# Attention scores and their maxima as products of 64 array rows, two heads side by side, in a fused attention and mixture-of-experts kernel

## What is computed

```
x = x + tanh(g_xattn) * attention(layernorm(x), ctx, ctx)
    scores = q_h . k_h / 4          (per head h, 256 x 77; keys beyond the query position masked)
    attn   = softmax(scores);  out = attn . v_h;  out @ W.T + b
x = x + tanh(g_ffn) * ffn(layernorm(x))
    shared = swiglu(x @ w_in.T) @ w_out.T
    h      = swiglu(x @ w1.T)
    routed = sum over the two chosen experts e:  (h * weight_e) @ w2[e].T
```

## Time and profile before

| | |
|---|---|
| median of 3 executions | 1141.14 us (1137.15 to 1141.66) |
| profiled execution | 1138.31 us, span of its instructions 1136.6 us |
| mean granted TensorE clock | 0.986 |
| PE busy | 1084.2 us, 95% of the span |
| weight loads busy | 908.4 us, 80% |
| DVE busy | 818.2 us, 72% |
| POOL busy | 520.0 us, 46% |
| ACT busy | 472.3 us, 42% |

### The profile page before, as it was taken

The page is one execution under the profiler, slowest core; times in us unless marked ns, Lnnn a source line. Parts: engine busy times, 40 slices in busy tenths (PEclk is TensorE's granted clock), DMA queues, the critical chain, the costliest instruction groups (busy, mean ns, idle before and its releaser), DMA issues.

```text
span 1136.6 us, 22381 instructions
## 1 busy us (share of the span) xinstructions
PE 1084.2 (95%) x7411; PEld 908.4 (80%) x7411; DVE 818.2 (72%) x1810; ACT 472.3 (42%) x722; POOL 520.0 (46%) x644
## 2 busy tenths in 40 slices
PE   5689999999999999999999999999999999999997
PEld 3467888888788787788888777888887888888886
DVE  7757786886876876877878676557544688888886
ACT  4565556555555555655555432233221111111111
POOL 5334447457357456465563534000001566666564
PEclk8989999999999999999999999999999899999999
DMA  8975748666765764766666112687652554555451
GB/s 157 244 159 120 147 102 129 135 126 102 146 137 123 119 146 106 113 141 128 99 128 145 29 55 74 209 260 242 214 173 104 163 157 154 163 166 150 148 175 64
DMA packets 106162, 160.64 MB, mean 141 GB/s; under 512 B 28828, under 2 KB 70718, under 8 KB 106048
## 3 DMA queue, kind: packets, MB, share of 16 engines
q1 hardware_dynamic: 94276, 121.18, 46.8%
q0 software_dynamic: 11776, 38.03, 11.1%
HBM read 75.24 MB, written 52.10 MB: 112 GB/s over the span
## 4 chain that ended last, share of the span: by engine, by line
PE 71%; issue 11%; DVE 7%; POOL 6%; DMA 3%; ACT 2%; SPq 1%; POOLq 0%; DVEq 0%; ACTq 0%
PE ps L764 16%; PE ps L811 12%; PE ps L709 7%; PE ps L726 7%; PE ps L813 6%; PE ps L631 4%; PE ps L796 3%; PE ps L619 3%; PE ps L662 2%; POOL tab_dram L1471 2%; PE ps L585 2%; PE ps L589 2%; POOL x L1447 2%; DMA regr<-regr 2%; PE ps L640 1%
## 5 line engine op out<-in xcount | busy, mean ns | idle before, releaser
L811 PE MATMUL ps<-regr,gh 128*128 x600 | 221.6, 407 | 0.2 <-issue 0.2
L888 ACT ACTIVATE Pt<-ps,pbias 77x1024 f32<-77x1024 f32 x128 | 141.6, 1106 | 98.2 <-PE ps L619 96.8
L813 PE MATMUL ps<-regr,gl 128*128 x600 | 170.0, 283 | 0.0
L811 PEld LDWEIGHTS ps<-regr,gh 128*128 128x128 f32 x600 | 113.8, 190 | 23.9 <-issue 0.6
L978 ACT ACTIVATE gh<-ps 128x512 fp32r<-128x512 f32 x75 | 44.8, 599 | 204.9 <-PE ps L796 204.9
L1189 DVE TENSOR_REDUCE mneg<-ps 128x8 f32<-128x616 f32 x128 | 100.4, 792 | 21.3 <-PE ps L589 21.1
L813 PEld LDWEIGHTS ps<-regr,gl 128*128 128x128 f32 x600 | 114.0, 190 | 0.0
L709 PE MATMUL ps<-x2h,winh 128*128 128x512 f32 x256 | 108.2, 423 | 0.6 <-DVE OHR L1093 0.6
L1379 POOL TENSOR_TENSOR gl<-gf,gh 128x512 fp32r<-128x512 f32 x64 | 82.7, 1293 | 42.8 <-ACT gh L850 42.6
L1447 POOL TENSOR_TENSOR x<-x,regf 128x512 f32<-128x512 f32 x32 | 41.1, 1285 | 132.7 <-DMA x<-in_x 132.7
L709 PE MATMUL ps<-x2h,winl 128*128 128x512 f32 x256 | 100.6, 393 | 0.0
(11 more groups left out here) (201 smaller groups left out, 2652.9 us busy)
## 6 DMA issues: line engine op xcount, KB each, us to landing
regr<-regr SPq DMA_DIRECT2D x96, 256.0 KB, 5.9
y_dram<-Pt SPq DMA_DIRECT2D x64, 256.0 KB, 2.4
regf<-in_x SPq DMA_DIRECT2D x32, 256.0 KB, 4.3
x<-in_x SPq DMA_DIRECT2D x32, 256.0 KB, 7.2
y_dram<-res SPq DMA_DIRECT2D x32, 256.0 KB, 2.4
regr<-regr SPq DMA_DIRECT2D x96, 77.0 KB, 6.9
x_dram<-x2h SPq DMA_DIRECT2D x14, 512.0 KB, 3.0
x_dram<-x2l SPq DMA_DIRECT2D x14, 512.0 KB, 3.8
```

The costliest lines, as they stand in the source:

```text
L811: e.matmul(o, gh2[:, k % 3, fc, :], w2v[:, bass.ds(val, 1), fc, :, :].rearrange("p o h d -> p (o h) d"), start=fc == 0, stop=False, skip_g ...
L813: m = e.matmul(o[:, 0, :], gl2[:, k % 3, fc, :], w2v[:, bass.ds(val, 1), fc, 0, :].rearrange("p o d -> p (o d)"), start=False, stop=fc == ...
L888: e.activation(Pt[0:K, 4 * k:4 * k + 4, :].rearrange("k (n j) t -> k n (j t)", n=2), bank_of["sc", b, k][0:K, :, :], ACT.Exp, bias=pbias[: ...
```

## The change

**Layout.** The 128 partitions are split into a lower and an upper half of 64, and head j of each pair lives in half j: `Kst` and `Xs` hold 50 rows from partition 64j (queries high, high, low in three blocks of 16, two rows of maxima), `Kbd` needs 4 instead of 8 heads per copy, and `mcat` is reordered.

**Maxima.** Each product has 64 rows (a half) and 308 columns; the two halves write separate banks. For the first half of the positions (k < 2) the mask still comes by the identity with 128 rows, now first; for k >= 2 it comes by `sel`, a matrix with a one in partitions 0 and 64, also in halves. A stage `mask` takes the banks, and waits for them, in slot 2k; `max` now stands in slot 2k+1, ahead of `scores`, and PE holds its products back until the causal masks of that `scores` stage are issued, so that products of 64 rows follow each other.

**Scores.** The four products of 100 rows become four of 50 rows, alternately in the lower and the upper half, the two heads in separate banks. ACT reads and writes in the new order, with one instruction as before.

**Transfers.** The three of `queries` become six, of half the size, the one of `maxT` becomes two. The ones in `Kst` are set once by POOL at the start, in place of a transfer with a copy on ACT and two clears on DVE.

```
-        put(i - 1, ((0, "max", 0), (0, "max", 1), (0, "max", 2), (0, "max", 3), (3, "maxT", 0)) if i < 6 else
-            ((0, "max", 0), (2, "max", 1), (4, "max", 2), (6, "max", 3), (9, "maxT", 0)))
+        put(i - 1, [(0, n, k) for k in range(4) for n in ("mask", "max")] + [(3, "maxT", 0)] if i < 6 else
+            [(2 * k + j, n, k) for k in range(4) for j, n in enumerate(("mask", "max"))] + [(9, "maxT", 0)])
...
                     for r, t in enumerate((xTh, xTh, xTl)):
-                        dst = Xs[32 * r:32 * r + 32, h, :, :, :].rearrange("p q c t -> p (q c t)")
-                        e.dma_start(dst.bitcast(F), t[:, h, :, :].bitcast(F)).then_inc(s[f"xs{h}"], 16)
+                        for j in range(2):
+                            o = 64 * j + 16 * r
+                            dst = Xs[o:o + 16, h, :, :, :].rearrange("p q c t -> p (q c t)")
+                            e.dma_start(dst.bitcast(F), t[64 * j:64 * j + 64, h, :, :].bitcast(F)).then_inc(s[f"xs{h}"], 16)
...
+            def maxima(b, k):
+                t, c = k // 2, k % 2
+                o = bank_of["mm", b, k][:, :, 0:4 * K].rearrange("p q (h k) -> p q h k", h=4)
+                if t:
+                    for j in range(2):
+                        e.matmul(o[:, j], sel[64 * j:64 * j + 64, :],
+                                 pad[64 * j:64 * j + 64, b, :].unsqueeze(1).broadcast_to([64, 4, K]), start=True, stop=False)
+                for j in range(2):
+                    m = e.matmul(o[:, j], xTh[64 * j:64 * j + 64, b % 2, c, t * P:(t + 1) * P],
+                                 Kbd[64 * j:64 * j + 64, b % G, c, :, :], start=False, stop=True)
+                m.then_inc(s["mm"], 1)
...
-                elif stage_ == "max":
+                elif stage_ == "mask":
...
                     bk, (sem, v) = take("P", "mm", b, k)
                     e.wait_ge(sem, v)
...
+                    if k < 2:
+                        for j in range(2):
+                            e.matmul(o[:, j], identb[:, :], first[:, h, :].unsqueeze(1).broadcast_to([P, 4, K]), start=True, stop=False)
+                elif stage_ == "max":
+                    if b < 5:
+                        maxima(b, k)
+                    else:
+                        maxima_due.append((b, k))
...
+                    while maxima_due:
+                        maxima(*maxima_due.pop())
                     for n in range(2):
-                        p, bk = 2 * k + n, pair[:, n, :]
+                        p = 2 * k + n
                         for j in range(2):
-                            m = e.matmul(bk[0:K, j * S:(j + 1) * S], Kst[:, ks, j, p % 4, 2 * g + p // 4, :],
-                                         Xs[:, h, p % 4, p // 4, :], start=False, stop=j == 1, skip_group_check=True)
+                            m = e.matmul(pair[0:K, j, n * S:(n + 1) * S], Kst[64 * j:64 * j + KR, ks, p % 4, 2 * g + p // 4, :],
+                                         Xs[64 * j:64 * j + KR, h, p % 4, p // 4, :], start=False, stop=n == 1, skip_group_check=True)
...
+            e.memset(sel[:, :], 0.0).then_inc(s["gcon"], 1)
+            e.wait_ge(s["gcon"], GCON["sel_zero"])
+            for j in range(2):
+                e.memset(Kst[64 * j + 32:64 * j + 64, :, :, :, :].bitcast(F), 1.0).then_inc(s["gcon"], 1)
...
-                    e.tensor_tensor(Kbd[:, b % G, k, :, :], khi[:, b % G * 2 + k, :].bitcast(F).unsqueeze(1).broadcast_to([P, 8, K]),
-                                    own8[:, :].unsqueeze(2).broadcast_to([P, 8, K]), ALU.mult).then_inc(s["kbd"], 1)
+                    e.tensor_tensor(Kbd[:, b % G, k, :, :], khi[:, b % G * 2 + k, :].bitcast(F).unsqueeze(1).broadcast_to([P, 4, K]),
+                                    own4[:, :].unsqueeze(2).broadcast_to([P, 4, K]), ALU.mult).then_inc(s["kbd"], 1)
```

More of the change, by code:

```diff
@@ L17 @@
 G = 2
-KR = 100
+KR = 50
 HID = 512
@@ L38 @@
 DCON = {n: i + 1 for i, n in enumerate(
-    "idb m8 ks0 va_zero va_one ones rec pre_zero pre wgh0 lb0 tgh brow pbias crow kcol ks1".split())}
-GCON = {n: i + 6 for i, n in enumerate("ident caus cauT upb kint".split())}
+    "idb m4 va_zero va_one ones rec pre_zero pre wgh0 lb0 tgh brow pbias crow kcol".split())}
+GCON = {n: i + 6 for i, n in enumerate("ident caus cauT upb kint sel_zero ones_low kst sel_low sel".split())}
 ROUTES = [(4 * c - 4, 8, c) for c in range(1, NCH - 2, 2)] + [(4 * c, 4, c) for c in (NCH - 2, NCH - 1)]
@@ L294, in build @@
         klo = carve(P, [2 * G, K])
-        Kbd = carve(P, [G, 2, 8, K])
+        Kbd = carve(P, [G, 2, 4, K])
         xTh = carve(P, [2, 2, S])
         xTl = carve(P, [2, 2, S])
-        w1_at = used[0]
+        w1_at = used[0] = max(used[0], 4096)
         kf = carve(P, [2 * G, K], regf)
@@ L574, in tensor @@
                     m.then_inc(s["xT"], 1)
-                elif stage_ == "max":
+                elif stage_ == "mask":
                     if k == 0:
                         e.wait_ge(s["xTh"], b + 1)
-                    t, c = k // 2, k % 2
-                    e.wait_ge(s["kbd"], 2 * b + c + 1)
+                        e.wait_ge(s["first"], b + 1)
+                    if b == 0 and k == 2:
+                        e.wait_ge(s["gcon"], GCON["sel"])
+                    e.wait_ge(s["kbd"], 2 * b + k % 2 + 1)
                     bk, (sem, v) = take("P", "mm", b, k)
@@ L582, in tensor @@
                     o = bk[:, :, 0:4 * K].rearrange("p q (h k) -> p q h k", h=4)
-                    for q in range(2):
-                        e.matmul(o[:, q], xTh[:, h, c, t * P:(t + 1) * P], Kbd[:, g, c, 4 * q:4 * q + 4, :], start=True, stop=False)
-                    if k == 0:
-                        e.wait_ge(s["first"], b + 1)
-                    for q in range(2):
-                        m = e.matmul(o[:, q], identb[:, :], (pad[:, b, :] if t else first[:, h, :]).unsqueeze(1).broadcast_to([P, 4, K]),
-                                     start=False, stop=True)
-                    m.then_inc(s["mm"], 1)
+                    if k < 2:
[6 more added lines that the diff above has]
+                        maxima_due.append((b, k))
                 elif stage_ == "maxT":
@@ L1404, in gpsimd @@
             e.iota(kint[:, :], pattern=[[0, 1]], base=0, channel_multiplier=1).then_inc(s["gcon"], 1)
+            e.memset(sel[:, :], 0.0).then_inc(s["gcon"], 1)
+            e.wait_ge(s["gcon"], GCON["sel_zero"])
+            for j in range(2):
+                e.memset(Kst[64 * j + 32:64 * j + 64, :, :, :, :].bitcast(F), 1.0).then_inc(s["gcon"], 1)
+                e.wait_ge(s["gcon"], GCON["ones_low"] + j)
+            for j in range(2):
+                e.memset(sel[64 * j:64 * j + 1, :], 1.0).then_inc(s["gcon"], 1)
+            e.wait_ge(s["gcon"], GCON["sel"])
             for stage_, b, k in order:
@@ L1538 @@
         _np.diff([p_[0] for p_ in pairs]), _np.diff([p_[1] for p_ in pairs])]).astype(_np.float32)
-    own = _np.zeros((4, 2, H, K), _np.float32)
-    for r_ in range(4):
-        own[r_, r_ % 2] = 1.0
-    arrays["own"] = own.reshape(4, -1)
     nc = _bacc.Bacc("TRN2", target_bir_lowering=False, num_devices=1)
```

70 lines of the change are left out of this document (28 added, 42 removed), and 2 rows, old and new, of the table names.

## The result

| | before | after |
|---|---|---|
| median | 1139.26 us (1135.84 to 1142.70, 6 runs) | 1198.27 us (1196.55 to 1200.22, 6 runs) |
| profiled execution, span | 1138.31, 1136.6 us | 1197.72, 1196.0 us |
| mean granted TensorE clock | 0.986 | 0.965 |

The ratio is 1.0501, 95% interval 1.0468 to 1.0534. The change costs 59 us. I had forecast 1170 us, with 1140 to 1190 as the range: the direction was right, the size was not, and the time lies outside the range.

The account below looks back on a forecast made before the run. Phase one looked bound by PE (494 of 500 us busy), with a late DVE reduction deciding. Profiled 1138.3 + 41 (waits) - 6 (PE) - 4 (values) + 2 (start) = 1171 us; predicted 1170, range 1140 to 1190.

Parts of the forecast that it names:

- forecast 0.8: PE's wait in slot 6 for the reduction of k = 2, in each of 13 iterations with `logits`: 0.8 us.
- My signs of being wrong: L584 starts without a wait, DVE's addition moves over 1 us against PE's slot 6, or pairs take twice as long.
- my sum of waits: PE's added waits for the reduction of k = 2 in slot 6: 29 + 10 + 2 = 41 us.
- The 10 us that I had for the iterations with `logits`: PE's waits in slot 6 of the 13 iterations with `logits`, 0.8 us each: 10 us.
- Transfers. I count nothing.: SP's four more issues for each batch, about 0.6 us each, counted at nothing; bytes ahead of the load stay the same.
- the load of x comes later: Rival on SP: load of x later by its 1.9 us of issues, in 12 iterations 23 us; 1190 us, chance 0.07.
- the ring: PE's products, result store, queries, load of x, POOL's bias, DVE's addition: the wait is paid in each such iteration.
- my 2.4: Mean PE wait in slot 6 of the 12 iterations without `logits`, all between 2.0 and 3.5 us: 29 us.
- halves do not overlap: Rival on PE: every product of half the rows costs a full one; 31 us more, about 1200 us, chance 0.06.
- -6 and +2: PE's saving behind the slot 6 wait, 0.23 us of k = 3 in 27 batches, -6 us; changed start, +2 us.
- The 4 us taken off for the values' waits: Low part of x stands ahead of DVE's fourth reduction, so the values' small waits for it shrink: 4 us off.
- 58 us by my estimate: Gain on PE from the skill's up to 2x alone: 32 x 1.8 us for each batch, 58 us.

Follow-up runs that it names:

- the filled idle time: Changed kernel, bank wait of k = 3 moved behind the transposes of x, and those transposes made seven times in iterations without `logits`: 1172.35 us, ratio 1.0254.
- the load between the queries: Changed kernel, with the load of x issued behind three of the six transfers of queries: 1143.38 us, ratio 1.0021.
- the run on order alone: Kernel before, full arrays and three transfers, only the products of the maxima one slot later: 1180.34 us, ratio 1.0311.
- the wait behind the transposes: Changed kernel, with PE's wait for the bank of k = 3 in slot 6 moved behind the transposes of x: 1184.72 us, ratio 1.0371.
- the remedies: Changed kernel with DVE's addition behind the reduction of k = 2 (iterations without `logits`), 1148.45 us; with the load of x ahead of the queries, 1140.91 us.
- the run with DVE's order alone: Kernel before, with only DVE's addition and its statistics put ahead of the reduction of k = 2, from the seventh iteration on: 1183.71 us, ratio 1.0356.

## Why the prediction was wrong

**Where it held.** The mechanism and the place: PE waits at the bank of k = 3, in slot 6, behind the addition, in twelve iterations of one kind and a little (0.4 us, forecast 0.8) in the others. It neither fades nor is paid once. My signs of being wrong did not fire either: the addition moved by 0.9 us against the transposes of the maxima, and I had allowed 1. The order in full arrays alone costs 37 to 44 us (two kernels, each against the runs of before beside it); my sum of waits was 41. That the two agree is luck in part. 12 waits of 2.6 us are 31. The 10 us that I had for the iterations with `logits` did not come (20.93 us against 20.88, so under 1 us in all). The clock, for which I had no term, costs about 12 by the filled idle time, and so stands in their place.

**The step that failed: "Transfers. I count nothing."** I had argued that the bytes ahead of the load of x hold it up and that they are the same. The bytes do count: the load between the queries showed it, 2 us for 384 KB. But the issues count too: I put them at nothing, and they cost 18 us. Full arrays with the moved order go from 1180.34 to 1198.33 us when the transfers are cut in two, 18 us (1.8% by the ratios, since the two were measured in different groups), and with the old order from 1142.6 to 1162.0, 19 us. I had the whole term in hand: 1.9 us later in 12 iterations, 23 us, with a chance of 0.07 as "the load of x comes later", 1190. It deserved far more. Two things in the rows spoke for it. The load is tied to PE's place by the ring that I had myself described from the store to the addition; a time inserted in a ring is paid in each turn. And POOL waited 2.63 us for the load, and DVE 1.68 us for POOL: each stood waiting for the one ahead, so what is added at the front can pass through. It does in part: the load was issued 2.0 us later against the transposes of the maxima (7.05 against 5.04) and the addition came 0.9 later. I had also charged it to the twelve iterations alone; in the run with the order and six issues, those with `logits` became 0.6 us longer as well (20.93 to 21.52), those without 0.7 (23.38 to 24.05). The Trainium skill, "DMA: Bandwidth & Descriptors" (Rules for kernel authors), advises one transfer in place of two to disjoint halves of the partitions, since both use the same 16 engines. I had not weighed it. The 18 and 19 us agree with its advice, but not for its reason: what the chain shows is the time of the issues on SP.

**The waits were longer than 2.4 us.** From the start of the last product to the next start it is 3.6 us in the mean, so some 3.2 idle. In the run on order alone it is 3.0, thus 2.6 idle, near my 2.4. The rest comes with the addition, which starts 14.3 us after the transposes of the maxima there and 14.8 after: the issues again.

**Clock.** I had no term for it. The trace of before had a clock of 1.00 in phase one, and the waits that I predicted were longer than any that it shows. The mean of 0.97 with the wait behind the transposes and 1.00 with the same place filled settles that it hangs on the idle time. The Trainium skill, "TensorE: Matmul & The Clock Gate" (HAM oscillation — how this bites in real kernels), tells of a loop whose wait in each turn sends the clock down each time; the stretches at half clock behind L584 agree. By its account half of the time at the lower clock is lost: an estimate of 14 us for the 27 us at half clock (100 to 600 us) in the kernel with the wait behind the transposes, where filling the place gave 12, and of 22 for the 44 us of the kernel after.

**PE's account.** The halves overlap, so the rival "halves do not overlap" (0.06), which gave 1200, is out although it was nearest to the time: right number, wrong mechanism. After and the full arrays with order and six issues differ by 0.06 us in the median. Within that, in the one trace of each, from batch 6 to 30 after is 4.1 us shorter (542.8 against 546.9), and its start is 3.5 us longer (batch 6 at 128.9 against 125.4 us). I had -6 and +2. The start is not settled by that: over the traces of all runs batch 6 comes anywhere from 123.8 to 133.2 us, in kernels with full arrays alone as well. The 4 us taken off for the values' waits did come, nearly: in these iterations PE stood 3.5 us ahead of the values before and never after. But 3.4 us of waiting for POOL ahead of the feed-forward's second products (L737) came in their place. The 2x of the Trainium skill, "TensorEngine Tiling (Array Packing)" (Theoretical Speedup), would have given 58 us by my estimate; with nearly every wait removed the measured gain is 7.

The account with measured terms: 1139.3 + 40 (order; with the clock in it) + 18 (issues) - 4 (halves) + 3.5 (start) = 1197, against 1198.3. The first two terms are medians of runs; the last two are read from single traces and nearly cancel.

**What stays open.** Whether the clock's 12 us hold for the kernel after as well was not measured; the idle time was filled in a kernel 14 us faster. And the remedies don't add up to the losses: each alone gives back 50 to 57 us of 59, since either one is enough to bring PE's wait to near nothing. How much of this is DVE's slack and how much the clock, no run tells. Nor was the full-array kernel with six transfers run with the load ahead of them, which would show whether the 18 us lie in the late load alone.

## What to carry to other kernels

- Count each DMA issue that a layout adds as time on its queue (0.6 us here), and look at what is queued behind it. If the last of the queue is what another engine waits for, and that chain comes back to the queue within one iteration, it can be paid in every turn: four more issues in an iteration cost 18 us here over the whole kernel. Put the transfer that someone waits for first: that one move was worth 57 us with the change and 10 us without.
- An engine that is busy for 99% of the time can hide a second chain that is as long. Before moving work on the busy engine, write down which instruction of the others becomes late; one addition and one reduction of DVE that change places cost as much as the whole moved order.
- A gain that is the difference between a saving (0.38 to 0.52 us) and a price (0.23 to 0.39 us) is worth little even if it is right. Here 7 us were left of 58 on paper.

## What the runs showed of the hardware

- Two products of 64 rows, or of 50, on the two halves of the array start 3 to 4 ns apart, two pairs of 256 columns 118 ns apart.
- A round trip from full products to halves and back costs about 0.23 us, from 0.92 us for four more stretches in a batch.
- A transfer of 128 KB takes SP as long to issue as one of 256 KB: 0.64 us (3.81 for six) and 0.63 (1.88 for three).
- A load of 256 KB lands 4.8 us after its issue with 384 KB of queries ahead of it, 7.3 us with 768 KB that took 1.9 us to issue. Where the same 768 KB went out as six transfers in 3.8 us, the load was issued 2.0 us later and landed 0.9 later: the longer issue is hidden in part.
- PE idle for 3 us in each second iteration has a stretch at 1.2 GHz at its end or right behind it each time, twelve of twelve, and so have the twelve waits of 1.8 to 2.5 us in the run with DVE's order alone. 2.6 us of work thrown away in the same place held it at 2.4 and made the kernel 12 us faster.
